# Moving the splitting of the third expert layer's weights from beside the second attention into the first two expert stages

## The chip, the cores and the metric

The program runs on one core of one Trainium2 chip. The metric is the device time of that core in microseconds (us). Before the change it was 2925.9 us, the median of three runs (2924.33 to 2934.3).

## The reference, cut to what matters

Eight sequences of 256 tokens with 256 channels (2048 tokens) go through four layers. Each layer is a gated cross-attention to 8 x 77 context rows and then a gated feed-forward with eight experts (sixteen in the last layer), of which every token uses two:

```
x = x + tanh(g_xattn[l]) * attention_l(layernorm(x), ctx)
x = x + tanh(g_ffn[l])   * experts_l(layernorm(x))

# attention 2 (the "second attention" of the change's words is layer index 2, eight heads of 128,
# each query against all 616 context rows), and the experts of layer index 2 ("third expert layer"):
h = silu(x @ gate_w[e].T) * (x @ up_w[e].T)        # 256 -> 704
y = sum over the two chosen e of w_e * (h @ down_w[e].T)
```

All matrix products are done in fp16 with two terms: every operand is split into a high and a low fp16 part, and a product is three matmuls (high x high, high x low, low x high). The inputs are fp32, so the weights have to be split on the chip too.

## The kernel before, in words

**Stages.** The program is a row of stages: the state-space and first attention, its convolution, an MLP, expert stage 0 ("moe0"), attention 1, expert stage 1 ("moe1"), attention 2, expert stage 2 ("moe2"), attention 3, and the last experts. PE, ACT and DVE meet at a barrier at the end of each; POOL (GpSimd) and SP (the DMA queue of SyncE) have programs of their own that run through `STREAM` and are tied to the others by semaphores only.

**Weight pieces.** Weights are cut into pieces of at most 2048 columns (`Piece`). A piece makes three steps. SP loads it as fp32 into `w_raw`, which has two halves used in turn (`load`, line 2532; it waits until POOL has split the piece two numbers earlier). POOL splits it (`split`): it scales it in place (line 2576), drains (2577), casts the high part (2579), drains (2580), subtracts for the low part (2582), and drains (2584). The result goes to `w_split` for attention and shared weights, or to `w_staged` (two slots in turn) for experts, from where SP stores it to the DRAM tensor `split_experts` (`store`, line 2539). POOL waits before a split until the piece has been loaded and until the store that last used its slot of `w_staged` has landed.

**An expert stage.** The tokens are sorted by expert into 23 tiles of 256 rows (`NTILE`). For every tile t, four queues have work:

- SP (lines 949 to 956) reads the tile's expert number and loads its split weights, 1.05 MB for the up projection after PE's and ACT's ups of tile t-2 are done, and 1.11 MB for the down projection after the downs of tile t-2. Then it calls a hook of t, which may load a weight piece.
- POOL (`SortedPool.rows`) gathers the 256 rows with two indirect DMAs (line 1089; it waits until PE has transposed tile t-2), then adds the result of tile t-3 to the residual rows in DRAM: a wait for DVE's output of that tile, a wait for the previous tile's additions to land, a one-element memset that gives DVE credit for its next output (line 1109), and two indirect DMAs (line 1112). Then it calls its hook, which may split a piece.
- PE transposes the gathered rows of tile t+1 in the middle of tile t (line 972), and does eight units of an up (985) and a down (1002) projection per tile.
- DVE and ACT make the hidden values, and DVE writes the tile's output (line 1061) once it has credit from line 1109.

**Where pieces are handled before the change.** In each of the first two expert stages four pieces of the next attention's weights are loaded at SP's tiles 3, 6, 9 and 12 and split three tiles later. The 32 pieces of the third expert layer are handled beside attention 2: for each of eight experts cuts of 1408, 1408 and 1280 columns and one piece of 64 rows x 256 columns. SP's queue in that attention issues two DMA transposes per step of one head (line 1739, 64 steps, called T below), and one load or one store of a piece after each step.

Of the kernel before, what the change touches and what calls it, by code (L numbers as in the profile page):

```python
# [67 lines left out]
J_X0, J_F0, J_X1, J_X2, J_X3, J_SH, J_E3 = 0, 1, 2, 4, 6, 7, 8  # L68


def build(nc, a, out):
    ctx = ExitStack()
    with ctx:
# [1048 lines left out]
        class Sparse:  # L1122
# [46 lines left out]
            def store(self, sp, s_):  # L1169
                sp.wait_ge(self.s_y, self.T0 + 2 + s_ + 1)  # L1170
                sp.dma_start(ysd[2 * s_ * P:2 * (s_ + 1) * P].rearrange("(k p) d -> p k d", p=P), self.ysb[:, s_ % 2])\
                    .then_inc(s_xr[s_ % 2], 16)
# [1258 lines left out]
        e0 = Sorted("moe0", [P] * 8, ACT.Relu, False, route(0))  # L2431
# [6 lines left out]
        e1 = Sorted("moe1", [P] * 8, ACT.Gelu, False, route(1))  # L2438
# [20 lines left out]
        e3 = Sparse(r3, e2)  # L2459
# [19 lines left out]
        def job_pieces(job, parts):  # L2479
            r = []  # L2480
            for n, (src, rows_, at) in enumerate(parts):
                w = src.shape[1]
                r.append(Piece(src, rows_, w, job=job, at=at, first=n == 0, last=n == len(parts) - 1).number)
            return r

        def halves(name):
            v = a[name]
            h = v.shape[1] // 2
            return [(v[:, 0:h], v.shape[0], 0), (v[:, h:2 * h], v.shape[0], h)]

        def expert_pieces(name, layer, cuts):

            r = []
            for e in range(8):
                for n, (c0, c1) in enumerate(cuts):
                    at = c0 + (8 if layer < 2 and n == 1 else 0)
                    r.append(Piece(a[name][e][:, c0:c1], P, c1 - c0,
                                   dram=wd[layer][e][:, at:at + c1 - c0]).number)
                if layer == 2:
                    r.append(Piece(a[name + "r"][e], 64, D, dram=wd[2][e][:, 4096:4096 + D]).number)  # L2500
            pieces[r[-1]].last_of_group = True
            return r

        HOOKS = {}
        full_cuts = [(0, 2048), (2048, 4096)]
        STREAM = job_pieces(J_X0, [(a["wx0"][:, 0:1280], P, 0), (a["wx0"][:, 1280:2304], P, 1280), (a["wx0c"], CP, 2304)])
        STREAM += ["film rows"] + job_pieces(J_F0, halves("wf0"))
        gates = {STREAM[-2]: 2, len(pieces): 2}
        pieces_before_experts = len(pieces)
        STREAM += expert_pieces("we0", 0, full_cuts) + [e0]  # L2510
        HOOKS[e0] = job_pieces(J_X1, halves("wx1")) + job_pieces(J_X1 + 1, halves("wx1c"))
        gates[len(pieces)] = n1.stage + 1
        BESIDE = {}
        BESIDE[a1] = expert_pieces("we1", 1, full_cuts)
        STREAM += [a1, e1]
        HOOKS[e1] = job_pieces(J_X2, halves("wx2")) + job_pieces(J_X2 + 1, halves("wx2c"))
        gates[len(pieces)] = n2.stage + 1
        BESIDE[a2] = expert_pieces("we2", 2, [(0, 1408), (1408, 2816), (2816, 4096)])
        STREAM += [a2, e2]
        HOOKS[e2] = job_pieces(J_X3, [(a["wx3"], P, 0), (a["wx3c"], CP, 2048)]) + job_pieces(J_SH, halves("ws3"))  # L2520
        for F, ps_ in HOOKS.items():
            HOOKS[F] = {3 + 3 * n: p for n, p in enumerate(ps_)}
        BESIDE[a3] = [Piece(a["we3"][e // 4][:, 768 * (e % 4):768 * (e % 4 + 1)], P, 768, dram=wd3[e]).number for e in range(16)]
        STREAM += [a3, e3]
        STORES = {e0: STREAM[STREAM.index(e0) - 1], e1: BESIDE[a1][-1], e2: BESIDE[a2][-1], e3: BESIDE[a3][-1]}

        def sp_piece(sp):
            def load(n):
# [69 lines left out]
        @block.sync  # L2598
        def _(sp):
            sp.dma_start(cst[:], a["cst"]).then_inc(s_const, 16)  # L2600
            sp.dma_start(xT[:].rearrange("p a b c -> p (a b c)")[:, 0:8 * D].bitcast(F32), a["s4"]).then_inc(s_const, 16)
            sp.dma_start(LDT, a["ldt"].partition_broadcast(P)).then_inc(s_const, 16)
            sp.dma_start(sc[:], a["sc"].partition_broadcast(P)).then_inc(s_const, 16)
            sp.dma_start(mk8[:], a["cmask"].partition_broadcast(P)).then_inc(s_const, 16)
            sp.dma_start(tm8[:], a["tmask"]).then_inc(s_const, 16)
            sp.wait_ge(s_zero, 1)
            sp.dma_start(dsk[0:P:16, :], a["dskip"]).then_inc(s_const, 16)
            sp.dma_start(b1c[:], a["b1"]).then_inc(s_const, 16)
            sp.dma_start(ctxr, a["ctx"]).then_inc(s_tmp, 16)
            sp.dma_start(xn[:, 0:2].rearrange("p a b -> p (a b)"), a["rows"][0:2 * D].partition_broadcast(P)).then_inc(s_tmp, 16)  # L2610
            sp.dma_start(frr[:, 0:2 * D], a["rows"][0:2 * D].partition_broadcast(33)).then_inc(s_tmp, 16)
            sp.dma_start(frr[:, 2 * D:6 * D], a["rows"][R_FI * D:(R_FI + 4) * D].partition_broadcast(33)).then_inc(s_tmp, 16)
            sp.dma_start(rwr, a["wr"]).then_inc(s_tmp, 16)
            sp.dma_start(b2r[0:17], a["b2"].rearrange("a (e n) -> (a e) n", n=D)).then_inc(s_tmp, 16)
            sp.dma_start(b2r[17:20], a["brow"].rearrange("(a n) -> a n", a=3)).then_inc(s_tmp, 16)
            sp.dma_start(x[:], a["x"]).then_inc(s_x, 16)

            def biases():
                sp.wait_ge(s_cdone, 1)
                for h in range(2):  # L2620
                    sp.dma_start(b2m[32 * h:32 * h + 1, 0, :], b2s[0:1, h]).then_inc(s_tmp, 16)
                    sp.dma_start(b2m[32 * h:32 * h + 1, 1:4, :], b2s[17:20, h]).then_inc(s_tmp, 16)
                cols = [wd[l][:, :, (N1[l] + 4096) // 2:(N1[l] + 4352) // 2] for l in range(2)]
                for l in range(2):
                    b1v = b1c[:, 8 + 64 * l:72 + 64 * l].rearrange("p (e n) -> p e n", e=8)
                    sp.dma_start(wd[l][:, :, 2048:2056].rearrange("e p n -> p e n"), b1v).then_inc(s_wdb, 16)
                    sp.dma_start(cols[l].rearrange("e p n -> p e n"), zeros.rearrange("p (e n) -> p e n", e=8)).then_inc(s_wdb, 16)
                sp.wait_ge(s_wdb, 64)
                for l in range(2):
                    for h in range(2):  # L2630
                        sp.dma_start(cols[l][:, 32 * h, :], b2s[1 + 8 * l:9 + 8 * l, h].bitcast(F32)).then_inc(s_wdb, 16)

            load, store = sp_piece(sp)
            for step_ in STREAM:
                if step_ == "film rows":
                    continue
                if step_ is e3:
                    e3.sp_part(sp)
                elif isinstance(step_, Sorted):
                    step_.sp_part(sp, lambda t: t in HOOKS[step_] and load(HOOKS[step_][t]))  # L2640
                elif isinstance(step_, Attn):
                    beside = BESIDE[step_]

                    def between(T):
                        per = 1 if step_ is a3 else 2
                        j = T // per + 2
                        if j < len(beside) and T % per == 0:
                            load(beside[j])
                        if T % per == per - 1 and j - 2 < len(beside):
                            store(beside[j - 2])  # L2650
                    for j in range(2):
                        load(beside[j])
                    AttnSP(step_, sp).run(between)
                    assert len(beside) <= step_.G * B // (1 if step_ is a3 else 2)
                else:
                    if step_ == pieces_before_experts:
                        biases()
                    load(step_)
                    store(step_ - 1)
                    if pieces[step_].last_of_group:  # L2660
                        store(step_)
            for s in s_end:
                sp.wait_ge(s, stage[0])
            sp.wait_ge(s_out, 64)

        @block.gpsimd
        def _(pool):
# [46 lines left out]
            for step_ in STREAM:  # L2714
                if step_ is e3:
                    e3.pool_part(pool)
                elif step_ == "film rows":
                    pool.wait_ge(s_end[2], 1)
                    film_rows()
                elif isinstance(step_, Attn):  # L2720
                    for n in BESIDE[step_]:
                        split(n)
                elif isinstance(step_, Sorted):
                    SortedPool(step_, pool).run(lambda t: t - 3 in HOOKS[step_] and split(HOOKS[step_][t - 3]))
                else:
                    split(step_)

# [89 lines left out]
```

## Time and profile before

The profiled execution took 2925.26 us, its span (first to last instruction) is 2923.5 us.

| Stretch of the span, us | stage | length, us |
|---|---|---|
| 757 to 800 | norm and routing of moe0 | 43 |
| 800 to 1090 | moe0, 23 tiles | 290 |
| 1106 to 1389 | attention 1 | 283 |
| 1389 to 1436 | norm and routing of moe1 | 47 |
| 1436 to 1722 | moe1, 23 tiles | 286 |
| 1722 to 1750 | norm before attention 2 | 28 |
| 1750 to 2133 | attention 2 | 383 |
| 2178 to 2488 | moe2, 23 tiles | 310 |

Over the whole span the busy shares are PE 70%, DVE 60%, ACT 41%, POOL 38%. They are means over stages that are limited by different things, so the stretches above have to be read one by one. In the rows, "issue" is time for which the profile shows no releaser, "POOLq" is an instruction of POOL's sequencer (a drain, for example), and "to landing" is the time from a DMA's issue until its data has arrived.

### The profile page before, as it was taken

The page shows a single profiled execution, that of the slowest core. Times are in us where ns is not written, and L with a number is a line of the kernel's source. Part 1 is how long each engine was busy: PE and PEld are TensorE (multiplying, and loading weights), DVE is VectorE, ACT ScalarE, POOL GpSimd, SP SyncE. Part 2 cuts the span into 40 slices and gives each one's busy share as a digit, 9 for nine tenths or more (in the row PEclk, how much of TensorE's full clock was granted, in tenths as well). Part 3 has the DMA queues.
Part 4 walks back from the last instruction along what each step waited for, and adds up shares of the span by engine and source line. Part 5 has one row for each costly group of instructions (what it writes and reads, how often), then busy time and mean ns, then how long its engine had stood idle before and what let it go on. Part 6 is the DMA issues. An engine that isn't in the chain of part 4 may idle for free.

```text
span 2923.5 us, 54934 instructions
## 1 busy us (share of the span) xinstructions
PE 2045.7 (70%) x18000; PEld 1580.0 (54%) x18000; DVE 1746.8 (60%) x4196; ACT 1203.1 (41%) x2798; POOL 1112.4 (38%) x1001
## 2 busy tenths in 40 slices
PE   0124556576199986886499968998849999584872
PEld 0112224543188864665388855776638887363461
DVE  6768872444733437786644446888765554677443
ACT  1112220032155645554366646667623443352341
POOL 4059700000046633563157522555404653240604
PEclk9956665588599997897699979999969999686996
DMA  4036407800368873776488746999947876353575
GB/s 121 0 81 230 172 0 215 245 1 0 123 207 233 243 204 98 200 206 166 140 262 254 224 124 127 221 225 236 217 141 214 243 225 170 95 154 91 109 242 165
DMA packets 430253, 484.29 MB, mean 166 GB/s; under 512 B 290145, under 2 KB 376731, under 8 KB 405597
## 3 DMA queue, kind: packets, MB, share of 16 engines
q1 hardware_dynamic: 355020, 394.72, 45.1%
q0 software_dynamic: 30336, 46.68, 9.1%
q10 hardware_dynamic: 44784, 41.55, 5.0%
q8 instruction: 51, 0.84, 0.1%
q14 instruction: 62, 0.50, 0.1%
HBM read 315.14 MB, written 100.61 MB: 142 GB/s over the span
## 4 chain that ended last, share of the span: by engine, by line
PE 49%; DVE 18%; DMA 9%; issue 8%; ACT 6%; DVEq 4%; POOL 2%; SPq 1%; ACTq 1%; PEld 1%; POOLq 0%; PEldq 0%
PE ps L985 14%; PE ps L1002 10%; PE ps L193 7%; PE ps L194 6%; PE ps L195 6%; DMA arena<-arena 3%; DMA arena<-s_kernel 2%; DVE bn_stats L236 2%; DMA residual_rows<-arena 1%; DVE arena L1676 1%; PE ps L295 1%; ACT arena L1644 1%; DVE arena L1844 1%; DVE arena L2235 1%; DMA w_split<-split_experts 1%
## 5 line engine op out<-in xcount | busy, mean ns | idle before, releaser
L985 PE MATMUL ps<-arena 128*128 128x256 f16 (+1 forms) x3864 | 512.1, 276 | 4.4 <-issue 4.4
L1053 DVE TENSOR_TENSOR arena<-ps,arena 128x256 f16<-128x256 f32 x506 | 214.3, 424 | 357.7 <-ACT arena L1031 353.4
L1002 PE MATMUL ps<-arena 128*128 128x256 f16 x3036 | 422.3, 273 | 0.0
L193 PE MATMUL ps<-arena 128*128 128x308 f16 (+6 forms) x1248 | 301.9, 268 | 167.7 <-DMA arena<-arena 34.5
L985 PEld LDWEIGHTS ps<-arena 128*128 128x128 f16 (+1 forms) x3864 | 376.9, 100 | 62.2 <-issue 15.0
L1089 POOL DMA_INDIRECT arena<-normed_rows,arena x138 | 142.2, 1030 | 669.9 <-DVEq L472 520.6
L2576 POOL TENSOR_SCALAR w_raw<-w_raw 128x1024 f32<-128x1024 f32 (+5 forms) x168 | 167.2, 1052 | 409.0 <-DMA split_experts<-w_staged 331.2
L1002 PEld LDWEIGHTS ps<-arena 128*128 128x128 f16 x3036 | 289.7, 98 | 48.2 <-DVE arena L1053 9.4
L194 PE MATMUL ps<-arena 128*128 128x308 f16 (+6 forms) x1248 | 301.2, 266 | 0.1
L195 PE MATMUL ps<-arena 128*128 128x308 f16 (+6 forms) x1248 | 300.1, 266 | 0.0
L2582 POOL TENSOR_TENSOR w_staged<-w_raw,w_staged 128x1024 f16<-128x1024 f32 (+3 forms) x136 | 252.6, 1874 | 12.0 <-issue 0.8
L1112 POOL DMA_INDIRECT residual_rows<-arena x138 | 221.5, 1605 | 60.1 <-issue 38.7
L193 PEld LDWEIGHTS ps<-arena 128*128 128x128 f16 (+3 forms) x1248 | 119.7, 104 | 226.3 <-issue 89.4
L1027 ACT ACTIVATE ps<-ps,arena 128x256 f32<-128x256 f32 x368 | 165.0, 448 | 182.6 <-PE ps L985 179.9
L1031 ACT ACTIVATE arena<-ps 128x256 f16<-128x256 f32 x506 | 194.2, 384 | 80.8 <-DVE ps L1051 68.7
L1676 DVE SCALAR_TENSOR_TENSOR arena<-ps,arena 128x512 f16<-128x512 f32 (+3 forms) x258 | 157.4, 633 | 112.7 <-ACT arena L1638 112.2
L295 PE MATMUL ps<-consts,arena 128*128 128x128 f32 x256 | 68.1, 415 | 198.1 <-DVE arena L258 184.2
L1638 ACT ACTIVATE arena<-ps 128x512 f16<-128x512 f32 (+3 forms) x258 | 141.6, 560 | 147.1 <-PE ps L195 142.5
L193 PE MATMUL ps<-w_split,arena 128*128 128x256 f16 x560 | 160.0, 286 | 4.0 <-DVE x_resid L811 2.7
L193 PE MATMUL ps<-xT,w_split 128*128 (+2 forms) x464 | 150.4, 324 | 14.4 <-DVE arena L1676 10.2
L194 PE MATMUL ps<-w_split,arena 128*128 128x256 f16 x560 | 159.6, 285 | 0.0
L195 PE MATMUL ps<-w_split,arena 128*128 128x256 f16 x560 | 159.1, 284 | 0.0
(315 smaller groups left out, 4511.5 us busy)
## 6 DMA issues: line engine op xcount, KB each, us to landing
arena<-split_experts SPq DMA_DIRECT2D x46, 1088.0 KB, 6.4
arena<-split_experts SPq DMA_DIRECT2D x46, 1028.0 KB, 5.4
w_raw<-in_we SPq DMA_DIRECT2D x32, 1024.0 KB
split_experts<-w_staged SPq DMA_DIRECT2D x32, 1024.0 KB, 4.6
arena<-s_kernel ACTq DMA_DIRECT2D x64, 512.0 KB, 5.0
arena<-split_experts SPq DMA_DIRECT2D x23, 1408.0 KB, 6.9
w_split<-split_experts SPq DMA_DIRECT2D x48, 384.0 KB, 4.2
arena<-split_experts SPq DMA_DIRECT2D x23, 768.0 KB, 4.4
```

The lines of the kernel that those rows point to most:

```text
L193: pe.matmul(out_ap, lhs(0), rhs(0), start=start, stop=False)
L194: pe.matmul(out_ap, lhs(0), rhs(1), start=False, stop=False)
L195: return pe.matmul(out_ap, lhs(1), rhs(0), start=False, stop=stop)
L985: last = pe.matmul(F.up_out(k, j, g), F.wu(k, a_, g, d, j), F.xe[:, k, b_, d * TROWS:(d + 1) * TROWS], start=g == 0 and d == 0 and n == 0, ...
L1002: last = pe.matmul(o, F.hh[0:m, F.part(k, j), a_, q * P:(q + 1) * P], F.wd(k, b_, m, j), start=j == 0 and n == 0 and q == 0, stop=j == F.N ...
L1027: act.activation(F.up_out(k, j, 0), F.up_out(k, j, 0), F.fn, scale=INV, bias=F.bias1(k, j))\
L1031: act.activation(F.hh[0:m, r, 0, :], F.up_out(k, j, 1 if F.gated else 0), ACT.Copy).then_inc(F.s_hhi, 1)
L1053: dve.tensor_tensor(F.hh[0:m, r, 1, :], hf, F.hh[0:m, r, 0, :], ALU.subtract).then_inc(F.s_h, 1)
L1112: pool.indirect_dma_start(xacc, bass.IndirectOffsetOnAxis(ap=F.route.to[:, n:n + 1], axis=0), F.ysb[:, k, q * D:(q + 1) * D], None, comput ...
L1676: m = dve.scalar_tensor_tensor(dst(1), view(A.bank(key)), scale, dst(0), ALU.mult, ALU.subtract)
L2576: pool.tensor_scalar(v, v, WSCALE, 1.0, ALU.mult, ALU.mult)
L2582: pool.tensor_tensor(to[:, 1, at + c0:at + c1], raw[0:height, n % 2, c0:c1], to[:, 0, at + c0:at + c1], ALU.subtract)
```

## The change

The 32 pieces of the third expert layer are handled in the first two expert stages: those of experts 0 to 3 in moe0, those of experts 4 to 7 in moe1, behind the four attention pieces that are handled there already. So each of the two stages has twenty pieces where it had four. In these two stages there is a piece in every tile: SP loads at t = 0 to 19, POOL splits at t = 1 to 20, one tile later instead of three, and SP stores the split piece two tiles after its load. Beside attention 2 nothing is left. In moe2 the five pieces keep SP's tiles 3, 6, ... 15 and are split one tile later instead of three.

```
-        BESIDE[a2] = expert_pieces("we2", 2, [(0, 1408), (1408, 2816), (2816, 4096)])
+        BESIDE[a2] = []
-        HOOKS[e0] = job_pieces(J_X1, halves("wx1")) + job_pieces(J_X1 + 1, halves("wx1c"))
+        HOOKS[e0] = job_pieces(J_X1, halves("wx1")) + job_pieces(J_X1 + 1, halves("wx1c")) + expert_pieces("we2", 2, cuts2, 0, 4)
-        HOOKS[e1] = job_pieces(J_X2, halves("wx2")) + job_pieces(J_X2 + 1, halves("wx2c"))
+        HOOKS[e1] = job_pieces(J_X2, halves("wx2")) + job_pieces(J_X2 + 1, halves("wx2c")) + expert_pieces("we2", 2, cuts2, 4, 8)
-            HOOKS[F] = {3 + 3 * n: p for n, p in enumerate(ps_)}
+            HOOKS[F] = {(n if F is not e2 else 3 + 3 * n): p for n, p in enumerate(ps_)}
...
-                    step_.sp_part(sp, lambda t: t in HOOKS[step_] and load(HOOKS[step_][t]))
+                    def tile_hook(t):
+                        if t in HOOKS[step_]:
+                            load(HOOKS[step_][t])
+                        if t - 2 in HOOKS[step_]:
+                            store(HOOKS[step_][t - 2])
+                    step_.sp_part(sp, tile_hook)
...
-                    SortedPool(step_, pool).run(lambda t: t - 3 in HOOKS[step_] and split(HOOKS[step_][t - 3]))
+                    SortedPool(step_, pool).run(lambda t: t - 1 in HOOKS[step_] and split(HOOKS[step_][t - 1]))
```

POOL in moe0, before: gathers of a tile, the memset and the additions, and a piece of an attention (`w_split`) in one tile of three.

```order
L1089 DMA arena<-normed_rows,arena 128x256 x2
L1109 MEMSET credit_dummy 1x1
L1112 DMA residual_rows<-arena 2304x256 x2
L2576 TENSOR_SCALAR w_raw<-w_raw 128x1024 x2
L2579 CAST w_split<-w_raw 128x1024 x2
L2582 TENSOR_TENSOR w_split<-w_raw,w_split 128x1024 x2
L1089 DMA arena<-normed_rows,arena 128x256 x2
L1109 MEMSET credit_dummy 1x1
L1112 DMA residual_rows<-arena 2304x256 x2
L1089 DMA arena<-normed_rows,arena 128x256 x2
```

POOL in moe0 after the change, at the first of the third expert layer's pieces (`w_staged`; the code has moved down by one line, so 2577, 2580 and 2583 are the lines 2576, 2579 and 2582 of before).

```order
L1089 DMA arena<-normed_rows,arena 128x256 x2
L1109 MEMSET credit_dummy 1x1
L1112 DMA residual_rows<-arena 2304x256 x2
L2577 TENSOR_SCALAR w_raw<-w_raw 128x1024
L2577 TENSOR_SCALAR w_raw<-w_raw 128x384
L2580 CAST w_staged<-w_raw 128x1024
L2580 CAST w_staged<-w_raw 128x384
L2583 TENSOR_TENSOR w_staged<-w_raw,w_staged 128x1024
L2583 TENSOR_TENSOR w_staged<-w_raw,w_staged 128x384
L1089 DMA arena<-normed_rows,arena 128x256 x2
L1109 MEMSET credit_dummy 1x1
```

In every tile from 1 to 20 a split now stands between the additions of one tile and the gathers of the next.

SP at the start of attention 2 before (`in_we2` is the raw third layer, `split_experts_2` its split form); after the change only the rows of line 1739 stay.

```order
L2532 DMA w_raw<-in_we2 128x1408 x2
L1739 DMA_TRANSPOSE arena<-arena 128x10x128 x2
L2532 DMA w_raw<-in_we2 128x1280
L1739 DMA_TRANSPOSE arena<-arena 128x10x128 x2
L2539 DMA split_experts_2<-w_staged 128x2x704
L1739 DMA_TRANSPOSE arena<-arena 128x10x128 x2
L2532 DMA w_raw<-in_we2r 64x256
```

SP in one tile of moe0 after the change (2533 is the load, 2540 the store). The load and the store stand behind the tile's weights and ahead of the next tile's.

```order
L953 DMA arena<-split_experts_0 128x2056
L956 ISA
L956 DMA arena<-split_experts_0 128x2176
L2533 DMA w_raw<-in_we2 128x1280
L2540 DMA split_experts_2<-w_staged 128x2x704
L949 TENSOR_LOAD arena
L949 ISA x2
L953 ISA
```

## Rows read from the trace of the kernel before

**Rows 1.** Stretches moe0, moe1, attention 2: busy us by engine, clock, DMA share
```profile
core 0: us, PE busy (x) PEld busy (x) DVE busy (x) ACT busy (x) POOL busy (x), PEclk, DMA share, GB/s
800.00:1090.00 290.00, 272.80 (x2410) 230.76 (x2410) 116.31 (x262) 166.91 (x391) 156.43 (x138) 0.96 0.77 224
1436.00:1722.00 286.00, 270.37 (x2410) 229.59 (x2410) 115.01 (x256) 168.19 (x392) 156.45 (x138) 0.97 0.77 221
1750.00:2133.00 383.00, 334.78 (x2654) 252.90 (x2652) 294.70 (x425) 250.20 (x473) 175.81 (x172) 0.99 0.88 198
```

**Rows 2.** Timeline of POOL in moe0, start and duration in us
```profile
804.10 1.29 POOL L1089 DMA_INDIRECT arena<-normed_rows,arena  x1 [0.30 <-issue]
...
838.27 0.09 POOL L1109 MEMSET credit_dummy<- 1x1 f32 x1 [5.22 <-DVE arena L1061]
...
861.38 0.09 POOL L1109 MEMSET credit_dummy<- 1x1 f32 x1 [5.18 <-DVE arena L1061]
...
863.54 1.57 POOL L1112 DMA_INDIRECT residual_rows<-arena  x1 [0.30 <-issue]
864.59 2.63 POOL L2576 TENSOR_SCALAR w_raw<-w_raw 128x1024 f32<-128x1024 f32 x2
869.16 2.02 POOL L2579 CAST w_split<-w_raw 128x1024 f16<-128x1024 f32 x2 [1.94 <-issue]
871.34 4.21 POOL L2582 TENSOR_TENSOR w_split<-w_raw,w_split 128x1024 f16<-128x1024 f32 x2 [0.15 <-issue]
876.38 1.07 POOL L1089 DMA_INDIRECT arena<-normed_rows,arena  x1 [0.84 <-PE ps L972]
...
878.74 0.09 POOL L1109 MEMSET credit_dummy<- 1x1 f32 x1
...
904.69 1.59 POOL L1112 DMA_INDIRECT residual_rows<-arena  x1 [0.30 <-issue]
905.73 2.66 POOL L2576 TENSOR_SCALAR w_raw<-w_raw 128x1024 f32<-128x1024 f32 x2
913.53 2.02 POOL L2579 CAST w_split<-w_raw 128x1024 f16<-128x1024 f32 x2 [5.14 <-issue]
...
1084.00 0.09 POOL L1109 MEMSET credit_dummy<- 1x1 f32 x1 [4.90 <-DVE arena L1061]
```

**Rows 3.** Chain of waits in moe0, 895 to 935 us: start, us, what
```profile
893.46 8.50 DMA residual_rows<-arena
...
908.39 5.14 issue
...
922.21 2.86 DMA arena<-normed_rows,arena
...
926.31 1.28 PE ps L985 x6
...
931.96 0.66 PE ps L1002 x6
```

**Rows 4.** POOL's additions in moe0 (tile residual_rows)
```profile
DMA to landing us min/median/max: 3.5/5.6/9.8
```

**Rows 5.** DMA in moe0: a queue's packets, MB, share; POOL's gathers, median us to landing
```profile
q1 hardware_dynamic: 7336, 54.88, 53.3%
...
arena<-normed_rows,arena POOLq DMA_INDIRECT x46, 4.5
```

**Rows 6.** Timeline of PE in moe0, transposes of the second tile
```profile
818.02 0.60 PE L972 MATMUL ps<-consts,arena 128*128 128x128 f32 x4
```

**Rows 7.** POOL's groups of instructions over the span, small shapes: busy, mean ns
```profile
L2582 POOL TENSOR_TENSOR w_staged<-w_raw,w_staged 128x256 f16<-128x256 f32 x16 | 16.6, 1037 | 1.2
L2579 POOL CAST w_staged<-w_raw 128x256 f16<-128x256 f32 x16 | 9.2, 574 | 1.1
```

**Rows 8.** Timeline of POOL in moe1
```profile
1439.91 0.96 POOL L1089 DMA_INDIRECT arena<-normed_rows,arena  x1 [0.30 <-issue]
...
1604.89 1.59 POOL L1112 DMA_INDIRECT residual_rows<-arena  x1 [0.30 <-issue]
...
1609.71 2.02 POOL L2579 CAST w_split<-w_raw 96x1024 f16<-96x1024 f32 x2 [1.12 <-issue]
...
1715.26 0.09 POOL L1109 MEMSET credit_dummy<- 1x1 f32 x1 [4.89 <-DVE arena L1061]
```

**Rows 9.** Chain of waits, 1722 to 2178 us (around attention 2), shares by line
```profile
by line: DMA arena<-arena 14.9%; issue 11.8%; PE ps L193 9.6%; PE ps L195 8.8%; PE ps L194 8.8%; ACT arena L1644 7.8%; ACTq L1648 5.1%; DVE arena L1686 4.2%; SPq L1739 3.7%; DVE arena L1676 2.8%; ACT arena L1660 2.7%; ACT arena L1638 2.5%; 
```

**Rows 10.** DMA issues, 1850 to 1950 us, then 2112 to 2125 us: median us to landing
```profile
arena<-arena SPq DMA_TRANSPOSE x38, 4.2
...
arena<-arena SPq DMA_TRANSPOSE x4, 3.5
```

**Rows 11.** DVE's line 1686, ns min/median/max, first and last start
```profile
L1686 DVE SCALAR_TENSOR_TENSOR arena<-arena x128: 841/917/2033, 1784.8 to 2116.8; 128x616 f16<-128x616 f32 x128
```

More of the change, by code:

```diff
@@ L2489, in halves, with expert_pieces @@
             return [(v[:, 0:h], v.shape[0], 0), (v[:, h:2 * h], v.shape[0], h)]
-        def expert_pieces(name, layer, cuts):
+        def expert_pieces(name, layer, cuts, first=0, end=8):
             r = []
-            for e in range(8):
+            for e in range(first, end):
                 for n, (c0, c1) in enumerate(cuts):
@@ L2505, in build @@
         full_cuts = [(0, 2048), (2048, 4096)]
+        cuts2 = [(0, 1408), (1408, 2816), (2816, 4096)]
         STREAM = job_pieces(J_X0, [(a["wx0"][:, 0:1280], P, 0), (a["wx0"][:, 1280:2304], P, 1280), (a["wx0c"], CP, 2304)])
@@ L2521, in build @@
         for F, ps_ in HOOKS.items():
-            HOOKS[F] = {3 + 3 * n: p for n, p in enumerate(ps_)}
+            HOOKS[F] = {(n if F is not e2 else 3 + 3 * n): p for n, p in enumerate(ps_)}
         BESIDE[a3] = [Piece(a["we3"][e // 4][:, 768 * (e % 4):768 * (e % 4 + 1)], P, 768, dram=wd3[e]).number for e in range(16)]
         STREAM += [a3, e3]
-        STORES = {e0: STREAM[STREAM.index(e0) - 1], e1: BESIDE[a1][-1], e2: BESIDE[a2][-1], e3: BESIDE[a3][-1]}
+        STORES = {e0: STREAM[STREAM.index(e0) - 1], e1: BESIDE[a1][-1], e2: HOOKS[e1][max(HOOKS[e1])], e3: BESIDE[a3][-1]}
         def sp_piece(sp):
@@ L2650, in between @@
                             store(beside[j - 2])
-                    for j in range(2):
-                        load(beside[j])
+                    for n in beside[0:2]:
+                        load(n)
                     AttnSP(step_, sp).run(between)
```

## The prediction, made before the changed kernel was run

> **What bounds the kernel now.** I read the stretches first, then the timeline of POOL in an expert stage, then the chain of waits there and around attention 2. The stretches show two kinds of stage [rows 1]. In moe0 and moe1 PE is busy for 272.8 of 290 us and 270.4 of 286 us: PE is the bound, and POOL, busy for 156 us, looks like an engine with 130 us to spare. In attention 2 PE is busy for 334.8 of 383 us, DVE for 294.7, and the DMA engines for 0.88 of the time; the chain of waits there passes through transposes made by DMA for 14.9% of its 456 us, which is 68 us, through their issue for 3.7% and through DVE's line 1686 for 4.2% [rows 9].
>
> The timeline of POOL tells more than its busy share. One tile without a split lasts 11.55 us (memsets at 838.27 and, two tiles on, 861.38) [rows 2]. A tile with a split of 2048 columns lasts from 861.38 to 878.74, 17.36 us. Only 8.9 us of that are the split's own instructions. What the busy share leaves out is the gap before the cast: the scaling ended at 867.2, and the cast starts at 869.16, 5.62 us after the second addition was issued at 863.54. At the next split the gap is 5.14 us, and the cast starts at 913.53, 8.84 us after the addition of 904.69. In moe1's last split it is 1604.89 to 1609.71, 4.82 us [rows 8]. The landing times of the additions are 3.5 to 9.8 us, median 5.6 [rows 4]. I read this as: the drain behind the scaling also waits until the additions issued just before have landed. The eight splits of the two stages give 4.8 to 8.84 us, mean 5.5. Before, a split came in one tile of three, so POOL caught up in the next two. Even so the split at 905 us put 8.5 us of an addition, the 5.14 us gap and a gather on the chain, and PE had to wait [rows 3].
>
> **The cost in moe0 and moe1.** Let L be the time from the second addition to the cast. A tile with 2048 columns takes 2.16 (memset to second addition) + L + 9.58 us (cast at 869.16 to the next memset at 878.74), that is 11.74 + L [rows 2]. In the 9.58 the cast and the subtraction are 2.02 + 4.21 = 6.23 us, which I scale by width: 4.28 us for 1408 columns and 3.89 us for 1280. For the small piece cast and subtraction are 0.57 + 1.04 us [rows 7], and some 0.9 us more for its memset and scaling, which stand behind the first drain (an estimate from these widths). The four iterations are then 9.8, 9.8, 9.4 and 8.1 us plus L, mean 9.3 + L. PE needs a tile each 11.55 us, so POOL becomes the bound when L is above 2.3 us, and no addition landed in under 3.5.
>
> L is the unknown. Below, it can be the 4.82 of moe1's last split; above, the 8.84, which came when a piece's load had just been issued behind the tile's weights. After the change each tile has such a load, and a store beside it. I take 6.9 us, between the mean of the eight and that case, nearer to the mean because the small pieces bring little traffic. So an iteration is 16.2 us.
>
> Now the timeline of moe0. POOL gathers tile 1 at 804.1 [rows 2]. The first four pieces (2048 columns) follow in tiles 1 to 4. Tiles 1 and 2 have no additions: second gather after 1.3, its landing 4.5 [rows 5], then cast to next gather 876.38 - 869.16 = 7.2, together 13 us each: tile 3's gathers start at 830.3. Tiles 3 and 4 take 17.4 each: tile 5's at 865.1. Tiles 5 to 20 take 16 x 16.2 = 259: tile 21's gathers start at 1124. Its rows land 6 us later, PE transposes them, and tile 22's 11.55 us after that. From a tile's transposes to the memset that shows its output is 838.27 - 818.02 = 20.25 us [rows 2, 6]. The memset of the last output comes at 865.1 + 259.2 + 6 + 11.55 + 20.25 = 1162.1, where it was 1084.0: **78 us later**. The slack of the start (tiles 1 to 4 run ahead of need) is in this sum already.
>
> The same for moe1: tile 1 at 1439.91, then 26 + 34.8 to 1500.7, + 259.2 + 37.8 = 1797.7 against 1715.26 [rows 8]: **82 us later**. Together 160 us. Each microsecond of L is worth 32 us: with L = 4.82 the sum is 94 us, with 8.84 it is 222 us.
>
> What the SP queue adds: its load at tile t waits for the split that POOL does at t-1, and the next tile's weights are queued behind it. In the lagging state POOL ends that split just as it starts tile t's gathers, and PE needs tile t+1's weights a whole iteration and 10 us later, so this wait costs nothing more. The added traffic is 17.6 MB in each stage: an expert's pieces are 2.16 MB to load and 2.23 MB to store, for four experts. Queue q1 moved 54.88 MB in 53.3% of 290 us [rows 5], 355 GB/s, so this is 50 us of all engines beside 0.77 x 290 = 223 us [rows 1], and 273 us fit into the longer stage; it costs through L alone. PE idles 4 to 5 us per tile. After such an idle time a group of six matmuls took 1.28 us instead of 0.66 [rows 3], the lower clock level of 1.2 GHz instead of 2.4. That penalty lies inside the same idle time, so I add 0; at most it is a few us per tile.
>
> **The gain in attention 2.** 32 loads and 32 stores leave SP's queue, POOL's 176 us go. The transposes took 4.2 us with that traffic and 3.5 at the end of the stage, where it has nearly stopped [rows 10]. A sixth to a quarter of 68 us is 11 to 17 us; a third of the 17 us of SP's issue time on the chain is 5 us. DVE's line 1686 takes 841 ns at least and 917 in the median, with singles at 2033 [rows 11]; of its 19 us on the chain about 3 go. As other waits move up, I take **20 us**. The lower bound is 0 (another wait replaces it; removed traffic gives no loss); the upper is PE's idle time, 383 - 334.8 = 48 us [rows 1], of which I leave a quarter to the stage's begin and end, so 36 us.
>
> The Trainium skill, "SBUF — State Buffer", section "SBUF: two separate sides", says that a DVE instruction with two SBUF inputs and a GpSimd instruction that reads SBUF lock each other out, whereas one with a single SBUF input doesn't contend. The spread of line 1686, 841 to 2033 ns with both inputs in SBUF, agrees [rows 11]. By that rule the instructions of DVE in moe0 and moe1 that read PSUM and one SBUF operand don't slow down there, and the whole gain on line 1686 comes back.
>
> In moe2 a split follows its load by one tile instead of three; POOL may wait some 5 us for the piece once or twice, under PE's work: 0, bounds 0 and 10.
>
> **Sum.** 2925.26 (the profiled execution, 1.76 us above its span and 0.6 below the median of the runs) + 160 - 20 = 3065 us, 3066 against the median.
>
> **The rivals.**
> - *The split hides behind PE, and the kernel gets faster.* This holds if the gap before the cast is not the wait for the additions, or goes away when each piece is small. Without it L is 1.05 us to the scaling's start plus 1.3 us per 1024 columns: 2.9, 2.9, 2.7 and 1.0, mean 2.4, so an iteration is 11.7 us, which is PE's pace. Nothing is lost in moe0 and moe1, the 20 us of attention 2 stay: 2905 us. For it speaks POOL's 130 us of spare time, against it that all eight gaps end when an addition could have landed. It decides from L = 2.3 us down.
> - *The loads and stores push L beyond 8.84* and the low clock comes on top: 222 us and more, without the gain: 3150 to 3200. For it, 9.8 us as the longest landing; against it, the rate per us hardly rises when the tile lengthens. The Trainium skill, "DMA: Bandwidth & Descriptors", section "Queues, rings and completion order", says that the DMA engines take turns between queues packet by packet. By it an addition on POOL's queue need not wait for all of SP's backlog, which speaks against this rival.
> - *The delay is smaller than summed*, as L stays at 4 or the pieces scale better than by width: 2 x 34 us, less 20 to 36: 2957 to 2975.
>
> **How the numbers follow.** The main case (L from 4.82 to 8.84; 2925 + 94 - 36 = 2983 to 2925 + 222 = 3147) has 0.76, the smaller delay 0.07, the larger 0.08, the rival of no loss 0.09. Single measurements of this kernel tell 0.3%, 9 us, from no change. Faster gets 0.07, within 0.3% 0.02, slower 0.91. The range is 2978 to 3148.
>
> **What would show it.** POOL's timeline in moe0: memsets 15 to 18 us apart from tile 5 to 20 (right) or 11.6 (wrong), casts that start 5 to 9 us after the second addition. PE would wait in moe0 and moe1 for gathers (line 972), DVE for the memset (line 1109), stages some 370 us long, PE busy for three quarters of them. Attention 2 at about 363 us, with transposes near 3.5 us. Wrong would be stages below 300 us, or waits of PE for the tile's weights instead.

## The result and the profile after

The changed kernel takes 3070.47 us, the median of four runs (3065.68 to 3080.73), against 2925.11 us before (four runs): a ratio of 1.0496, 95% interval 1.0465 to 1.0526. It is slower by 145 us. The profiled execution has a span of 3069.5 us against 2923.5.

The first rows are the stretches of moe0, moe1 and attention 2, with the columns of [rows 1].

```profile
core 0: us, PE busy (x) PEld busy (x) DVE busy (x) ACT busy (x) POOL busy (x), PEclk, DMA share, GB/s
799.00:1166.00 367.00, 292.40 (x2410) 240.17 (x2410) 114.77 (x261) 166.66 (x391) 234.95 (x226) 0.89 0.75 225
1514.00:1886.00 372.00, 296.27 (x2410) 241.95 (x2410) 113.92 (x256) 167.96 (x392) 234.99 (x226) 0.90 0.73 213
1914.00:2280.00 366.00, 330.06 (x2656) 253.40 (x2654) 264.32 (x425) 250.30 (x474) 0.00 (x0) 1.00 0.64 115
```

The two expert stages have grown by 77 and 86 us, attention 2 has shrunk by 17. PE does the same 2410 matmuls in an expert stage and is now idle for a fifth of it. POOL has 79 us more to do in each, and that is all that busy shares say: 235 us of 367, a third of the stage to spare. The DMA engines move about as much per second as before. No engine looks like the bound; the timeline shows which one is. For exact lengths I take the start of each norm's statistics (DVE's line 236), the first work of a stage:

| from norm to norm, us | before | after | difference |
|---|---|---|---|
| moe0 with its routing | 337.1 | 414.6 | +77.5 |
| attention 1 | 295.5 | 297.2 | +1.7 |
| moe1 with its routing | 335.6 | 422.1 | +86.5 |
| attention 2 with its norm | 408.1 | 390.7 | -17.5 |
| moe2 with its routing | 357.7 | 357.7 | 0.0 |

The timeline of POOL in moe0, as in [rows 2]. The code has moved by one line: 2577 is the scaling, 2580 the cast, 2583 the subtraction.

```profile
884.28 0.09 POOL L1109 MEMSET credit_dummy<- 1x1 f32 x1
...
886.53 1.57 POOL L1112 DMA_INDIRECT residual_rows<-arena  x1 [0.30 <-issue]
887.58 2.10 POOL L2577 TENSOR_SCALAR w_raw<-w_raw 128x1024 f32<-128x1024 f32 x2
895.95 1.49 POOL L2580 CAST w_staged<-w_raw 128x1024 f16<-128x1024 f32 x2 [6.27 <-issue]
897.59 3.00 POOL L2583 TENSOR_TENSOR w_staged<-w_raw,w_staged 128x1024 f16<-128x1024 f32 x2
903.79 0.09 POOL L1109 MEMSET credit_dummy<- 1x1 f32 x1
...
906.03 1.57 POOL L1112 DMA_INDIRECT residual_rows<-arena  x1 [0.30 <-issue]
907.07 2.00 POOL L2577 TENSOR_SCALAR w_raw<-w_raw 128x1024 f32<-128x1024 f32 x2
910.02 1.38 POOL L2580 CAST w_staged<-w_raw 128x1024 f16<-128x1024 f32 x2 [0.95 <-issue]
...
1125.02 0.09 POOL L1109 MEMSET credit_dummy<- 1x1 f32 x1
...
1160.12 0.09 POOL L1109 MEMSET credit_dummy<- 1x1 f32 x1 [3.18 <-DVE arena L1061]
```

From 884.28 to 903.79 is one iteration, 19.5 us. Within it the cast starts 9.4 us after the second addition was issued, with a gap of 6.27 us that has no releaser. In the next iteration the same distance is 4.0 us. The last memset is at 1160.12, where it was 1084.00 [rows 2].

What the others wait for in moe0 (in total, times, longest), of the changed kernel:

```profile
PE ps L972 <- DMA arena<-normed_rows,arena: 67.0, 13, 9.8
...
DVE arena L1061 <- POOL credit_dummy L1109: 50.2, 11, 8.2
POOL w_staged L2580 <- issue: 43.3, 12, 6.9
```

PE waits for gathered rows and DVE for POOL's memset. Both stand behind a split in POOL's program. No wait of PE for a tile's weights is among them.

And the chain of waits around attention 2 (1886 to 2327 us), which answers to [rows 9], with DVE's line of [rows 11] under it:

```profile
by line: PE ps L193 13.9%; PE ps L195 12.8%; PE ps L194 12.8%; issue 11.7%; ACT arena L1644 10.5%; ACTq L1648 6.9%; DMA arena<-arena 5.1%; ACT arena L1638 3.2%; ACT arena L1660 3.2%; DVE arena L1676 1.7%; DVE bn_stats L236 1.7%; DMA x_resid
...
L1686 DVE SCALAR_TENSOR_TENSOR arena<-arena x128: 847/851/858, 1950.3 to 2265.0; 128x616 f16<-128x616 f32 x128
```

The transposes' share fell from 14.9% to 5.1%, PE's matmuls rose in its place, and line 1686 takes 851 ns each time, where it had reached 2033 with POOL at work.

### The profile page after: what moved, and what is told of

Same layout as the page of the kernel before. It is cut to its first block, busy times and chain, and to the rows that moved or that the text cites. A ratio compares the mean times of both kernels' runs of the same rounds, so it can differ in the third digit from the quotient of the medians.

```text
span 3069.5 us, 54934 instructions
## 1 busy us (share of the span) xinstructions
PE 2088.0 (68%) x18000; PEld 1602.1 (52%) x18000; DVE 1709.3 (56%) x4196; ACT 1201.3 (39%) x2798; POOL 1089.2 (35%) x1001
## 4 chain that ended last, share of the span: by engine, by line
PE 32%; DVE 16%; issue 16%; POOL 12%; DMA 7%; ACT 6%; DVEq 4%; POOLq 3%; ACTq 2%; PEld 1%; SPq 1%; PEldq 0%
PE ps L193 7%; PE ps L194 7%; PE ps L195 7%; PE ps L985 6%; POOL residual_rows L1112 4%; PE ps L1002 3%; DMA residual_rows<-arena 2%; POOL arena L1089 2%; POOL w_raw L2577 2%; POOL w_staged L2583 2%; DVE bn_stats L236 2%; ACT arena L1644 2%; POOLq L2585 1%; DMA arena<-arena 1%; DMA arena<-s_kernel 1%
## 5 line engine op out<-in xcount | busy, mean ns | idle before, releaser
L985 PE MATMUL ps<-arena 128*128 128x256 f16 (+1 forms) x3864 | 531.5, 282 | 4.4 <-issue 4.4
L1002 PE MATMUL ps<-arena 128*128 128x256 f16 x3036 | 437.2, 280 | 0.0
L985 PEld LDWEIGHTS ps<-arena 128*128 128x128 f16 (+1 forms) x3864 | 386.5, 102 | 70.9 <-issue 15.0
L1002 PEld LDWEIGHTS ps<-arena 128*128 128x128 f16 x3036 | 297.8, 100 | 56.2 <-DVE arena L1053 9.4
L2583 POOL TENSOR_TENSOR w_staged<-w_raw,w_staged 128x1024 f16<-128x1024 f32 (+3 forms) x136 | 244.2, 1812 | 12.0 <-issue 0.9
L193 PE MATMUL ps<-xT,w_split 128*128 (+2 forms) x464 | 150.9, 325 | 13.9 <-DVE arena L1676 9.6
```

Source lines behind the costliest of these rows:

```text
L193: pe.matmul(out_ap, lhs(0), rhs(0), start=start, stop=False)
L985: last = pe.matmul(F.up_out(k, j, g), F.wu(k, a_, g, d, j), F.xe[:, k, b_, d * TROWS:(d + 1) * TROWS], start=g == 0 and d == 0 and n == 0, ...
L1002: last = pe.matmul(o, F.hh[0:m, F.part(k, j), a_, q * P:(q + 1) * P], F.wd(k, b_, m, j), start=j == 0 and n == 0 and q == 0, stop=j == F.N ...
L2583: pool.tensor_tensor(to[:, 1, at + c0:at + c1], raw[0:height, n % 2, c0:c1], to[:, 0, at + c0:at + c1], ALU.subtract)
```

## The experiments

My theory: POOL's iteration of a tile is the bound of moe0 and moe1, since the drain in a split waits until the additions issued just before have landed. Rival A: the loads and stores of the pieces cost the time. Rival B: POOL's arithmetic does. The first four runs take these apart. Percentages are ratios to the kernel before in the same session and on the same chip. The kernel before has medians of 2921.6 us (e1, e2, e3, e5), 2975.4 (e4, e6, e7, e8; another chip) and 2925.5 (e9, e10, e11), so only ratios and stage lengths are compared. On that other chip the difference lies behind the last norm alone, 308.7 us in e4 where the trace of before has 260.3; the earlier stages that an edit leaves alone agree within some us. The stage lengths come from one profiled execution each.

**e1: the changed kernel without drains in the splits.** Each instruction of a split raises a semaphore, and POOL waits for that in the drain's place (shortened, with comments of mine):

```
-                pool.drain()                       # behind the scaling; the same behind the cast
+                passed()                           # pool.wait_ge(s_sp, number of split steps so far)
...
-                pool.drain().then_inc(s_pc, 1)
+                passed()
+                pool.memset(spare[:, 61:62], 0.0).then_inc(s_pc, 1)
```

> The changed kernel, with POOL's drains between scaling, cast and subtraction of every piece replaced by waits on a semaphore that the split's own instructions raise; loads, stores and places of all pieces stay. Theory (the drain behind the scaling waits until the additions just issued have landed): an iteration of POOL falls from 15.9 us to its instructions, 2.25 + 1.04 + scaling + cast to next memset, about 12 us, close to PE's 11.55; moe0 and moe1 end within 10 us of before's, attention 2 keeps its gain of 17.5 us: 2905 to 2930 us. Rival A (the loads and stores of the pieces are what lengthens the two stages): unchanged, above 3040 us. Rival B (POOL's arithmetic itself is too much): 3040 us or more.

Measured: 2950.39 us, ratio 1.0101 (1.0080 to 1.0121); stages moe0 +12.4, moe1 +21.7, attention 2 -13.9 us. Four fifths of the 4.96% are gone although every load, store and arithmetic instruction is still there. That is above my 2930: the two stages still lose 34 us. POOL's timeline in moe0 of e1 (2590 scaling, 2593 cast, 2596 subtraction):

```profile
878.41 1.57 POOL L1112 DMA_INDIRECT residual_rows<-arena  x1 [0.30 <-issue]
879.46 2.10 POOL L2590 TENSOR_SCALAR w_raw<-w_raw 128x1024 f32<-128x1024 f32 x2
881.62 1.49 POOL L2593 CAST w_staged<-w_raw 128x1024 f16<-128x1024 f32 x2
883.19 3.00 POOL L2596 TENSOR_TENSOR w_staged<-w_raw,w_staged 128x1024 f16<-128x1024 f32 x2
```

The cast follows the scaling at once, 3.2 us after the second addition, and no addition of moe0 landed in under 3.5 us in this run (median 7.1).

What is left of the loss has two parts. The first is POOL's pace, which I had put too low with "about 12 us":

```profile
863.46 0.09 POOL L1109 MEMSET credit_dummy<- 1x1 f32 x1
...
1062.69 0.09 POOL L1109 MEMSET credit_dummy<- 1x1 f32 x1 [3.09 <-DMA residual_rows<-arena]
```

These are tiles 5 and 21, so an iteration takes 12.45 us (12.6 in moe1) where PE needs 11.55. The second is a late start, which e3 shows.

**e2: the kernel before without drains in the splits** (the same edit).

> The kernel before with the same replacement of drains by waits on a semaphore, as the base for the run beside it. Theory: before, the gaps fell in one tile of three and POOL caught up, so only the one stall of PE in moe0 (about 4 to 6 us) can go: 2918 to 2925 us. Rival A and B: 2925 us, no change.

Measured: 2916.60 us, ratio 0.9986 (0.9973 to 0.9998), and once more in a later session (e11) 2913.12 us, ratio 0.9963 (0.9948 to 0.9977):

> The kernel before with the semaphores alone once more, on the same chip as the half move, so that the two can be compared: ratio 0.997 to 0.9995.

moe0 is 6.8 us shorter in e2: the stall of [rows 3] is gone. The run beats both kernels, the one before by 0.1 to 0.4%. That the stall went because of the edit isn't shown: e8 below keeps all drains, and its moe0 is 6.8 us shorter too.

**e3: the traffic alone.** The third layer's splits return before any arithmetic:

```
+                if name_of(p) == 2:                # (mine: one of the 32 pieces in moe0 and moe1)
+                    col = 29 + sorted(third).index(n)
+                    pool.memset(spare[:, col:col + 1], 0.0).then_inc(s_pc, 1)
+                    return
```

> The changed kernel with all loads and stores of the third layer's pieces in moe0 and moe1, but without POOL's scaling, cast, subtraction and drains for them (only a one-element memset that raises the count), so the third layer's split weights are not computed. Theory: with the traffic alone POOL's iteration is some 7 to 9 us, below PE's pace; moe0 and moe1 are within 10 us of before's and attention 2 is 17 us shorter: 2905 to 2925 us. Rival A (traffic is the cost): 3040 us or more. Rival B (POOL's arithmetic): 2905 to 2925 us.

Measured: 2927.17 us, ratio 1.0018 (1.0002 to 1.0033); moe0 +7.7, moe1 +10.4, attention 2 -17.0 us. The time is 2 us above my range. Rival A as the main cause is out. Yet the two stages are 18 us longer, as much as attention 2 gains. POOL waits for stores there:

```profile
895.94 0.09 POOL L2563 MEMSET credit_dummy<- 1x1 f32 x1 [6.33 <-DMA split_experts<-w_staged]
```

But such waits don't reach PE. Its transposes (line 972) of the seventh and of the last tile of moe0 are:

```profile
887.70 0.60 PE L972 MATMUL ps<-consts,arena 128*128 128x128 f32 x4
...
1072.56 0.60 PE L972 MATMUL ps<-consts,arena 128*128 128x128 f32 x4
```

That is 16 tiles in 184.9 us, PE's own 11.55 us each, with all loads and stores beside them; moe1 has the same 184.9. The loss falls ahead of the seventh tile. There the changed kernel, and e3 with it, splits the four attention pieces one behind the other, where the kernel before has three tiles from one to the next. The chain of waits in e3 from 804 to 875 us runs through these four splits and the gaps of their drains:

```profile
805.78 2.08 POOL w_raw L2586 x2
807.86 2.97 issue
...
855.50 2.11 POOL w_raw L2586 x2
857.61 2.94 issue
```

Counted from the norm, the sixth tile's transposes come 9.9 us later than before in moe0 and 8.8 in moe1. In e5 below, which places these four pieces alike but has no load and store of the third layer in the two stages, they come 8.6 and 5.3 us later. So most of the 18 us is the crowded start; the traffic's own part is at most a few us, and these runs don't give it exactly.

**e5: POOL's work alone.** The kernel before, with the four attention pieces in tiles 1 to 4 and the arithmetic and the drains on scratch contents in tiles 5 to 20, without a load or a store for them.

```
+                        elif step_ is not e2 and 5 <= t <= 20:
+                            work((t - 5) % 4)      # 1408, 1408, 1280, 256 columns, drains as in split
```

> The kernel before, with the four attention pieces at the changed kernel's tiles, and in tiles 5 to 20 of moe0 and moe1 the same scaling, cast, subtraction and drains as in the changed kernel but on scratch contents, with no load and no store; the third layer is still handled beside attention 2. Theory: additions land in 4 to 5.6 us without the traffic, POOL's iteration is 14 to 14.5 us, so moe0 and moe1 together lose some 100 us, attention 2 gains nothing: 3010 to 3045 us. Rival A (traffic is the cost): 2925 to 2935 us. Rival B (arithmetic): 3040 us or more.

Measured: 3003.92 us, ratio 1.0283 (1.0256 to 1.0310); moe0 +38, moe1 +43 us, attention 2 unchanged. A little less than I had put: additions land faster without the traffic (median 3.9 us), and L is 4.4 us in moe0 and 4.6 in moe1.

**e6: the same work without drains** (edits of e5 and e1 together).

> As the run with POOL's arithmetic alone in tiles 5 to 20 of moe0 and moe1 (3004 us, no loads, no stores), with the drains of that arithmetic and of all splits replaced by waits on a semaphore. Theory: an iteration is about 12 us, mostly hidden: 2922 to 2940 us, so some 70 us of the 82 were the wait of the drain. Rival B (POOL's arithmetic is too much): 2990 us or more.

Measured: ratio 1.0043 (1.0022 to 1.0064). Of the 2.83% of e5, 2.4 points went with the drains. They include those of all other splits, worth 0.1 to 0.4 points in the kernel before (e2, e11). Rival B as the main cause is out: the arithmetic and the crowded start together cost 0.43%, or 0.6 to 0.8% against e2 and e11, which have no drains either.

**e4: the traffic and a single drain.** As e3, with `pool.drain().then_inc(s_pc, 1)` in the memset's place.

> As the run with the traffic alone (2927 us), but each of the third layer's pieces in moe0 and moe1 now has a single drain on POOL and nothing else; the third layer's split weights are again not computed. Theory (a drain waits for the additions issued before it): the gathers of the next tile can't be issued before the additions have landed, so an iteration becomes 2.25 + L + about 3.3 us, with L near 7 some 12.5 us instead of about 8; that is 1 us above PE's pace, and moe0 and moe1 lose 5 to 20 us each against the run with the traffic alone: 2935 to 2965 us. Rival (the gap before the cast is not the drain's wait but something of the arithmetic): 2922 to 2932 us, no difference to the traffic alone.

Measured: ratio 1.0246 (1.0213 to 1.0279) against 1.0018 without the drain; moe0 +36, moe1 +45 us. Here no arithmetic stands between an addition and the next gather, so the wait can be read by itself:

```profile
879.91 1.59 POOL L1112 DMA_INDIRECT residual_rows<-arena  x1 [0.30 <-issue]
889.89 1.02 POOL L1089 DMA_INDIRECT arena<-normed_rows,arena  x1 [8.39 <-issue]
...
894.45 1.58 POOL L1112 DMA_INDIRECT residual_rows<-arena  x1 [0.30 <-issue]
904.66 1.02 POOL L1089 DMA_INDIRECT arena<-normed_rows,arena  x1 [8.63 <-issue]
```

One drain keeps POOL idle for 8.4 and 8.6 us. I had expected an L near 7 and 5 to 20 us a stage; with iterations of up to 15.6 us in moe0 and 16.1 in moe1 it is 28 and 34 us a stage above e3. The direction was right, the size was not: L isn't a constant.

**e9 and e10: half of the move.** Eight pieces in each of moe0 and moe1, in every second tile, sixteen left beside attention 2; e9 with drains, e10 without.

```
-            HOOKS[F] = {(n if F is not e2 else 3 + 3 * n): p for n, p in enumerate(ps_)}
+            HOOKS[F] = {((0, 1, 2, 4, 6, 8, 10, 12, 14, 16, 18, 20)[n] if F is not e2 else 3 + 3 * n): p for n, p in enumerate(ps_)}
```

> Half of the move, with the drains as in the changed kernel: the third layer's experts 0 and 1 (8 pieces) in moe0, 2 and 3 in moe1, in every second tile only (SP's tiles 6, 8, ... 20), the attention pieces at 0, 1, 2 and 4; experts 4 to 7 stay beside the first half of attention 2. Theory: POOL's pace decides, and two tiles take one iteration with a split (15.9 us) and one without (6.5 to 9.5), together 22.4 to 25.4 us against PE's 23.1, so the loss is far less than half of the changed kernel's 164 us: 5 to 25 us in moe0 and moe1 together, attention 2 gains 6 to 10 us, ratio to before 0.999 to 1.006. Rival A (the traffic itself costs) or any cost per piece: half of the 4.96%, ratio about 1.025.

> The same half of the move with the drains of all splits replaced by waits on a semaphore. Theory: POOL's two tiles then take about 12 + 6.5 = 18.5 us, no bound; what is left is the traffic, 18 us for 32 pieces in the two stages, so some 5 us for 16, against 6 to 10 us of gain in attention 2 and the 4 us that the semaphores give to the kernel before: ratio to before 0.994 to 0.999, the best version if the sum holds. Rival (traffic costs the same per piece anywhere): 0.999 to 1.003.

Measured: e9 1.0212 (1.0183 to 1.0240), e10 1.0018 (0.9999 to 1.0037). Both are misses. In e9 moe0 loses 28 and moe1 38 us, attention 2 gains 9. I had counted on POOL catching up in the tile without a split. It does so only at times:

```profile
885.36 0.09 POOL L1109 MEMSET credit_dummy<- 1x1 f32 x1
...
901.26 0.09 POOL L1109 MEMSET credit_dummy<- 1x1 f32 x1
...
913.16 0.09 POOL L1109 MEMSET credit_dummy<- 1x1 f32 x1 [5.46 <-DMA residual_rows<-arena]
```

The tile with the split took 15.9 us as expected, the next one 11.9 us: the wait ahead of the memset, for the previous tile's additions to land, takes over from the drain. Half of the pieces bring 43% of the loss. That is nearer to the 1.025 of the rival, a cost per piece, than to my range; but e10 has the same traffic and arithmetic, so 1.9 of the 2.1 points are the drains'. In e10 moe1 is still 10.4 us longer, and moe0 9 us longer than in e11. In moe0 all of that stands ahead of the eighth tile: the start is crowded here too. So even without the drains the move gains nothing over e11. A version that leaves the four attention pieces where they were was not run.

**e7 and e8: beside the MLP and the convolution.** The trace of before shows no POOL work from 450 to 757 us and no DMA traffic from 575 to 757 us. All 32 pieces follow those of the first layer, from the end of the convolution (e7) or at once (e8):

```
+        gates[len(pieces)] = 4                     # e7: behind the convolution; 2 in e8
+        early = expert_pieces("we2", 2, [(0, 1408), (1408, 2816), (2816, 4096)])
+        STREAM += early + [e0]
```

> The kernel before with all 32 pieces of the third layer handled right behind those of the first layer, from the end of the convolution (575 us) on, beside the MLP, where the trace of before shows neither DMA traffic nor POOL work; nothing in moe0, moe1 or beside attention 2; drains as before. Theory: some 6 us a piece, 200 us, so the splits end near 770 us and delay nothing of moe0 that is needed before 791; attention 2 gains its 17.5 us. The norm behind the MLP (705 to 757 us) has DVE instructions with both inputs in SBUF, which can lose 0 to 25 us to POOL's. Sum 2904 to 2930 us. Rival (DVE's two-input instructions lose more than attention 2 gains): 2930 to 2950 us.

> The same without the wait for the end of the convolution: the third layer's pieces follow the first layer's at once (from some 450 us), beside the convolution, and end near 650 to 680 us, before the norm behind the MLP. Theory: the norm is free of POOL, attention 2 gains 17.5 us, the convolution, whose own loads keep the DMA engines 0.90 busy, loses 0 to 20 us: 2904 to 2925 us. Rival (DMA contention beside the convolution costs more than the gain): 2930 us or more.

Measured: e7 1.0075 (1.0053 to 1.0097), e8 1.0066 (1.0040 to 1.0092): both a little worse than before, and both misses, at what their rivals had said. Attention 2 gained 16.9 and 17.8 us as expected. In e7 the MLP's stretch lost 17.1 us and the norm behind it 18.6 us; POOL's last split ended at 779.7 us, inside that norm. Why the MLP lost its 17 us I have not taken apart. DVE's lines in that norm, of before and then of e7 (min/median/max):

```profile
L2371 DVE TENSOR_TENSOR xn<-xn,arena x16: 424/425/426, 716.4 to 755.6; 128x256 f32<-128x256 f32 x16
```

```profile
L2371 DVE TENSOR_TENSOR xn<-xn,arena x16: 425/568/2201, 733.9 to 790.8; 128x256 f32<-128x256 f32 x16
```

In e8 the norm is untouched, but the stages before it, whose own loads keep the DMA engines busy (0.90 of the time from 450 to 575 us before), lost 31 us.

## Why the prediction was right

**The bound.** POOL's iteration sets the pace of moe0 and moe1. Shown: tiles 5 to 20 take 254.9 us between the memsets of 870.13 and 1125.02, 15.9 us each, where I had 16.2, and none of these iterations has a wait for another engine ahead of its memset. In moe1 it is 16.3.

**The wait of the drain.** Shown by e1, e6 and e4, each of which changes the drains alone beside the same traffic or arithmetic. Taking them out is worth 3.9 points of 4.96 in the changed kernel and 2.4 of 2.83 in the work alone; adding one costs 2.3 points. The trace of the changed kernel shows it directly too. The second additions of two of its tiles, issued at 886.53 and at 906.03, took:

```profile
DMA to landing us min/median/max: 9.1/9.1/9.1
...
DMA to landing us min/median/max: 3.7/3.7/3.7
```

The casts started 0.3 us after these landings, at 895.95 and 910.02. Of the 36 splits behind additions in the two stages, the cast starts 0.29 us after the later landing in 28, and 0.85 us in the eight small pieces, whose scaling also stands behind the first drain. In e1 the casts of the third layer's pieces start 3.7 to 8.0 us before it, wherever the trace has the landing. The first rival, a split hidden behind PE, was to decide from L = 2.3 us down; the shortest L was 4.0.

**The size of L.** I took 6.9 us out of 4.82 to 8.84. Measured over tiles 5 to 20 it is 6.8 us in moe0 and 7.2 in moe1. It isn't a steady 7: in moe0 it is either 4.0 to 5.1 or 8.5 to 10.0. It is long where the second addition was issued at most 4.6 us after the load of the tile's down weights (line 956), with the piece's load and store behind that, and short where it was issued 6.9 us after it or more. That the mean came to 6.9 is in part luck, as I had taken one middle value. Without the pieces' traffic (e5) it is 4.4 and 4.6 on average. So the traffic works through L, and about half of the loss needs it: e5 has 81 us of the 164, and 2.4 and 2.6 us less L in 16 tiles make up 80 us of the rest.

**The sums.** moe0 +78 predicted, the last memset came 76.1 us later; moe1 +82, measured +86.5 from norm to norm. The late start was in the timeline: tile 5's gathers were to come at 865.1, and came at 867.8. Attention 2 -20, measured -17.5; here the sum was right and not its terms. The transposes' landing fell to 3.5 us as said, but on the chain they fell from 68 to 22 us, not by 11 to 17, and PE's matmuls rose from 124 to 174 us. moe2 0, measured 0.0. Together 140 against 145 us. The scaled instruction times were a little off in both directions: the cast and subtraction of 1408 columns took 1.49 + 3.00 = 4.5 us where I had 4.28, those of the small piece 1.1 us where I had 1.6.

**What I left at nothing.** The penalty of the lower clock fits into PE's waits: the mean granted clock of moe0 fell from 0.96 to 0.89, between the levels of 1.2 and 2.4 GHz, and PE's busy time rose by 20 us, without a sign of it in POOL's pace. The wait of SP's loads for POOL cost nothing either, as PE waited for gathers and not for weights. The prediction doesn't say what the late start is worth by itself: 5 to 10 us a stage (e3, e5), most of what attention 2 gains. In the changed kernel it is a small part of the loss; it decides as soon as the drains are gone, together with POOL's 12.45 us a tile.

**The rule on the shared port** (the Trainium skill, "SBUF — State Buffer", section "SBUF: two separate sides") held where I used it: in moe0 DVE's lines 1053, 1061 and 1043, with one input in SBUF, took 423, 477 and 692 ns on average, 424, 475 and 691 before, beside 79 us more of POOL; line 1686 with two came back to 851 ns. The section excepts instructions in a 2-port mode from what I wrote of a single input; none of these three shows a slowdown.

## What to carry to other kernels

An engine with a third of its time idle can still be the bound, if its program is a chain of short steps with waits in it: add up one iteration from marker to marker, waits included, and compare it with the iteration of the engine that it feeds. Where a GpSimd queue carries both DMAs and arithmetic, order the arithmetic with semaphores on its own instructions and not with drains. And before work is moved into a stage because an engine is idle there, see what it crowds together at the stage's start, before POOL has any lead; here that cost about as much as attention 2 gained.

## What the runs showed of the hardware that I had not expected

- A GpSimd drain behind an indirect DMA waits for that DMA's data to land, not only for its issue: 8.4 and 8.6 us of idle time with nothing but the drain between an addition and a gather (e4), none with a semaphore in its place (e1).
- In moe0 of the changed kernel the cast starts 4.0 to 5.1 or 8.5 to 10.0 us after the second addition, never between; in moe1 5 of 16 lie between. The same addition takes twice as long when it is issued just behind 1.1 MB of weights, a load and a store of another queue.
- DVE's tensor_tensor of 128x256 fp32 with both inputs in SBUF took up to 2201 ns instead of 425 beside POOL's splits (e7).
